# Attention 0: the input normalised by ScalarE at the head of its step, the key parts written to DRAM one step later

## The reference, cut to what matters

```python
def _layernorm(x, axis=-1, eps=1e-05):
    m = jnp.mean(x, axis=axis, keepdims=True)
    v = jnp.var(x, axis=axis, keepdims=True)
    return (x - m) / jnp.sqrt(v + eps)
...
    q = (x @ Wq).reshape(B, N, NUM_HEADS, HEAD_DIM).transpose(0, 2, 1, 3)
    k = (context @ Wk).reshape(B, M, NUM_HEADS, HEAD_DIM).transpose(0, 2, 1, 3)
    v = (context @ Wv).reshape(B, M, NUM_HEADS, HEAD_DIM).transpose(0, 2, 1, 3)
    attn = jax.nn.softmax(jnp.einsum('bhnd,bhmd->bhnm', q, k) * scale, axis=-1)
    out = jnp.einsum('bhnm,bhmd->bhnd', attn, v)
    return out @ Wo + bo
...
x = x + _L0_xattn_ref(_layernorm(x, axis=-1), ctx_1024, ...)
```

## Time and profile before

| | us |
|---|---|
| median of three runs | 829.3 (825.61 to 832.38) |
| profiled execution, its own time | 826.71 |
| span in it, first to last instruction | 824.3 |
| PE busy | 543.9 (66%) |
| DVE busy | 524.3 (64%) |
| ACT busy | 414.7 (50%) |
| POOL busy | 297.6 (36%) |

### The profile page before, as it was taken

The page is one execution under the profiler, slowest core; times in us unless marked ns, Lnnn a source line. Parts: engine busy times, 40 slices in busy tenths (PEclk is TensorE's granted clock), DMA queues, the critical chain, the costliest instruction groups (busy, mean ns, idle before and its releaser), DMA issues.

```text
span 824.3 us, 19004 instructions
## 1 busy us (share of the span) xinstructions
PE 543.9 (66%) x5619; PEld 357.2 (43%) x5619; DVE 524.3 (64%) x1608; ACT 414.7 (50%) x1037; POOL 297.6 (36%) x559
## 2 busy tenths in 40 slices
PE   5788889847888678887322432799996138793352
PEld 4576667634544454554101211455564026561131
DVE  2767676645777557776788885466775853326673
ACT  2666667733222236665435764565563014445674
POOL 2444444424555423342024326344430023323510
PEclk9999999978999759999555555599999557876555
DMA  8832333310000033432000001233330015550001
GB/s 228 212 69 62 67 64 64 69 31 0 1 0 0 18 79 91 113 96 59 10 1 0 0 0 40 53 88 89 91 91 17 0 39 142 133 137 2 0 0 52
DMA packets 102629, 47.51 MB, mean 58 GB/s; under 512 B 82160, under 2 KB 92080, under 8 KB 102448
## 3 DMA queue, kind: packets, MB, share of 16 engines
q1 hardware_dynamic: 102576, 46.87, 22.6%
HBM read 26.92 MB, written 19.92 MB: 57 GB/s over the span
## 4 chain that ended last, share of the span: by engine, by line
issue 29%; PE 20%; DVE 17%; POOL 12%; ACT 5%; DVEq 5%; DMA 5%; POOLq 3%; SPq 2%; ACTq 0%
PE bank L510 3%; DMA scratch_q<-q_parts 3%; PE bank L444 3%; POOL small L1362 2%; PE bank L459 2%; PE bank L551 2%; DMA stacks<-scratch_q 2%; POOL tmp_a L1250 2%; DVE xn L1604 2%; POOL stats L1222 2%; PE bank L476 1%; DVE small L1445 1%; DVE mx L1628 1%; PE bank L590 1%; POOL tmp_b L1250 1%
## 5 line engine op out<-in xcount | busy, mean ns | idle before, releaser
L1628 DVE TENSOR_REDUCE mx<-bank 128x4 f32<-128x512 f32 x160 | 103.8, 683 | 22.0 <-PE bank L459 20.3
L909 ACT ACTIVATE probs<-bank 128x512 f32<-128x512 f32 x160 | 90.9, 595 | 48.3 <-PE bank L480 46.2
L1283 POOL CAST q_parts<-resid 128x128 bf16<-128x128 f32 x48 | 14.2, 296 | 94.8 <-DVE resid L1643 94.8
L1643 DVE SCALAR_TENSOR_TENSOR resid<-bank,w_bias_cols,q_parts 128x128 f32<-128x128 f32 x48 | 16.8, 350 | 49.2 <-ACT q_parts L959 49.2
L510 PE MATMUL bank<-probs,v_slot 128*9 128x128 f32 x1024 | 45.9, 299 | 3.0 <-ACT probs L909 0.8
L1222 POOL TENSOR_TENSOR stats<-stats,half_neg 128x1 f32<-128x1 f32 x48 | 26.2, 546 | 57.3 <-DVE stats L1599 57.1
L1109 ACT ACTIVATE att_t<-bank 128x512 f32<-128x512 f32 x16 | 9.6, 597 | 63.8 <-PE bank L780 63.8
L476 PE MATMUL bank<-stacks 48*128 48x128 bf16 x512 | 39.6, 228 | 1.9 <-DVE shift_t L1664 1.1
L480 PE MATMUL bank<-shift_t,pick_bf 64*128 64x128 bf16 x512 | 39.4, 227 | 0.3 <-issue 0.3
L546 PE MATMUL bank<-w_ident,xn 128*128 128x128 f32 x64 | 21.4, 334 | 27.0 <-DVE xn L1604 15.8
L982 ACT ACTIVATE att<-bank 128x512 f32<-128x512 f32 (+1 forms) x48 | 25.1, 522 | 23.3 <-PE bank L510 21.5
(11 more groups left out here) (298 smaller groups left out, 1756.6 us busy)
## 6 DMA issues: line engine op xcount, KB each, us to landing
stacks<-scratch_k SPq DMA_DIRECT2D x64, 96.0 KB, 2.2
stacks<-scratch_q SPq DMA_DIRECT2D x64, 96.0 KB, 2.2
scratch_k<-k_parts SPq DMA_DIRECT2D x48, 96.0 KB, 1.9
scratch_q<-q_parts SPq DMA_DIRECT2D x48, 96.0 KB, 1.9
scratch_k<-k_parts SPq DMA_DIRECT2D x48, 64.0 KB, 1.7
scratch_q<-q_parts SPq DMA_DIRECT2D x48, 64.0 KB, 1.7
stacks<-scratch_k SPq DMA_DIRECT2D x16, 192.0 KB, 2.6
stacks<-scratch_q SPq DMA_DIRECT2D x16, 192.0 KB, 2.5
```

Source lines behind the costliest of these rows:

```text
L909: activation(probs[:, slot, :], bank[2 + u % 2][:, :], ACT.Tanh if layer == 3 else ACT.Exp, scale=float(d) ** -0.5).then_inc(sm["p"], 1)
L1628: reduce(mx[:, sM, at * UNIT:(at + 1) * UNIT], bank[u % 2][:, :].rearrange("p (h k) -> p h k", h=UNIT), AX.X, ALU.max).then_inc(sm["mx"], 1)
```

## The change

Four edits, all in attention 0:

- SP: in step t the nine writes are those of sequence t-2 instead of t-1, behind a wait for `kk_parts` of t-1 instead of t; one more emptying step is run.
- DVE: `xn_ready` is gone from the step.
- ACT: `normalized_input` is issued first in the step, ahead of `key_copied`.
- POOL: `deviation` computes for attention 0 what it does for 1 and 2 (negated mean, power, drain, product) instead of the power alone. DVE's `ln_stats` gets the wait that keeps a slot of `stats` until ACT has read it.

```diff
--- before.py
+++ after.py
@@ -325,17 +325,18 @@
                 if on(k, 0) and k >= SLOTS:
                     wait(sp, L0x["v_ps"], t - SLOTS + 1)
                     context(t, k)
-                if on(k, 1):
-                    s = (k - 1) % SLOTS
-                    wait(sp, L0x["kk_parts"], t)
+
+                if on(k, 2):
+                    s = (k - 2) % SLOTS
+                    wait(sp, L0x["kk_parts"], t - 1)
                     for l in range(3):
                         row = 0
                         for part, n in TERMS:
-                            sp.dma_start(scratch_k[l, t - 1, row:row + n].rearrange("j r k -> r j k"),
+                            sp.dma_start(scratch_k[l, t - 2, row:row + n].rearrange("j r k -> r j k"),
                                          k_parts[:, s, l, 0:n, :]).then_inc(k_saved[s], 16)
                             row += n
 
-            pipeline(sp, contexts, 1)
+            pipeline(sp, contexts, 2)
@@ -984,6 +985,7 @@
                     if layer == 0:
+                        normalized_input()
                         key_copied()
@@ -1227,7 +1229,7 @@
                     def deviation(t, k):
-                        if layer in (0, 3):
+                        if layer == 3:
                             rstd(2 * layer, t, k)
                             return
@@ -1590,7 +1592,7 @@
-                if half in (2, 4):
+                if half in (0, 2, 4):
                     wait(dve, ln["xn"], half // 2 * B + t - 3)
@@ -1705,7 +1707,6 @@
                         maximum(0)
-                        xn_ready()
                         maximum(1)
```

## The result

| | before | after |
|---|---|---|
| median of 13 runs each, us | 831.61 (825.61 to 838.76) | 835.79 (833.73 to 838.04) |
| ratio, 95% interval | | 1.0055 (1.0036 to 1.0073) |
| span of the profiled execution, us | 824.3 | 834.2 |

The kernel became slower, by 0.55%; the medians lie 4.2 us apart. That is inside the stated range. The loss is clear of the interval's scatter but small, and it is less than half of the 10.1 us that were worked out. The two profiled executions differ by 9.9 us of span, more than twice as much as the medians.

The account below looks back on a forecast made before the run. In attention 0 PE was nearest to full but waited for contexts; after the change ACT's head would wait for POOL. Steady steps +6.4 and first steps +3.7 gave +10.1 us, forecast 838 between two bases, range 827 to 843.

Parts of the forecast that it names:

- What bounds the stage: Attention 0: PE nearest to full, busy 18.3 of 21 us, waiting 10.4 us in nine steps for the late context.
- the SP edit: SP's writes in attention 0: context issued earlier, PE's wait vanishes; alone worth 0 to 9.7 us, moved writes cost nothing.
- the chain to ACT's head: Attention 0: ACT's head waits through DVE and POOL for its own line 1017; line 970 at +4.13, steady loss 6.4 us.
- The first piece of a step: Attention 0, ACT's line 1017 to line 977: 4.53 us in every step, where it was 3.95 on the mean.
- the old mean step: Attention 0 before the change: eleven steps in 108.27 us, mean 9.84, set against a forecast step of 10.42.
- the last two: Pieces of a step, line 977 to 945 and 945 to the next 1017: together 5.89 us, holding in every step.
- the first steps: Steps 0 to 4 of attention 0: delays summing to +3.7 us, bounds 0 and 4.5.
- what follows: Everything after attention 0: starts after it and moves as a whole.
- Faster: Rival, attention 0: ACT never held at its head, every step 8.96 us; gain 9.7 us, 817 or 820; chance 0.10.
- No change: Rival: first steps' 3.7 us hidden behind loads, or new path nearer its low bound; 827 to 836 us; chance 0.25.
- the forecast's +6.4 to +13: Main case: steady loss in attention 0 plus first-step delays, worked out at +10.1 us; chance 0.58.
- Slower still: Rival, POOL in attention 0: later products slip too, 0.57 us paid twice per step, 6.3 more, 844 us; chance 0.07.

Follow-up runs that it names:

- earlier statistics: Changed kernel with DVE's next-sequence statistics moved just behind the shifts and POOL's deviation ahead of its products, except every fourth sequence: 821.39 us, ratio 0.9881.
- with the earlier statistics added: Kernel before with the SP edit plus DVE's statistics and POOL's deviation moved earlier, DVE still normalising: 819.5 us, ratio 0.9852.

## Why the prediction was right in sign and too large

**What bounds the stage, the SP edit, the chain to ACT's head: right.** The first piece of a step was forecast at 4.53 and is 4.53; the step at 10.42 and is 10.39; ACT's idle time at its head at 2.7 and is 2.73. The SP edit alone is worth 818.5 against 829.59, 11.1 us, where the gap of the profiled execution gave 9.7 as an upper bound; the base was short, as below. The loss is the wait on `ln_rstd`. Taking its cause away (earlier statistics) makes the kernel 8.2 us faster than the one before on the same chip (821.39 against 829.59), moving it back in ACT's queue 2.9 (826.73 against 829.59), where the changed kernel is 4.2 slower: 12.4 and 7.0 us of its time come back.

**The rule on engine load.** The Trainium skill, Perfetto Trace Analysis, Optimizing Scalar/DVE Operations, says that moving work off DVE may make sense if DVE is saturated. The prediction read from it that here the move buys nothing, and the traces agree: DVE is busy 7.6 us less (524.3 to 516.7 on the page of the profile), and with the wait taken away the steps last 9.00 us with the move and 8.95 without it. That by engine load alone it would cost nothing either is the prediction's reading, not the page's words, and it misses the 12.4 us that the order of the queues took (the gain of the earlier statistics).

**The term that was mis-sized: the old mean step.** The prediction set 10.42 against 9.84, which is the mean of one execution, and that was a short one. Against 10.19, the mean in both later profiles, the steady steps lose (10.39 - 10.19) x 11 = 2.2 us, not 6.4; against the mean of all three profiles 3.4. The prediction's sentence that only the first piece of a step varies, with the last two at 5.89, holds for that one execution: in the five steps behind which the clock fell, the last two take 6.55 to 7.50 us. The changed kernel's step doesn't vary, since nothing in its loop waits for a DMA; the old one's did. The spread of the three runs then at hand, 825.6 to 832.4, beside a step that varied from 8.96 to 10.90 in one trace, could have said so: the prediction noted the 2.6 us to the median and split the difference, but left the step at 9.84.

**The sum by all five profiles.** On the mean of three profiles of before and two of after the steady steps cost +3.4 us, the first steps +3.2, and what follows -1.9: +4.7 us of span, beside the 4.2 us between the medians. The prediction had what follows move as a whole; it varies by 6.3 us from profile to profile, more than the change itself, so this last term may be chance.

**Luck in the time.** That 838 lies only 2.2 us above the measured 835.79 is luck. The change was 5.9 us smaller than worked out, but the base of about 828 was 3.7 below the 831.61 that thirteen runs gave, and the two errors offset each other.

**The first steps: near on the mean, but not in step 4.** Forecast +3.7 by line 1017 of step 4 (50.05 in the earlier trace rows). The first profile of after has it at 55.49, +5.4, the second at 53.41, which is +1.5 and +1.7 against the second and third profile of before; the means differ by 3.2. Steps 1, 2 and 3 came as forecast: +0.87, +0.45 and +1.25 in the second profile of after, against 0.87, 0.45 and 1.05. Where the clock fell in step 1, in the first profile, that step added 2.2 (last section). Step 4 was forecast at +0.84. It took 14.17 and 14.13 us in the changed kernel, with the clock at 0.50 for part of it, and in the kernel before 12.99 where the clock held, but 14.49 and 14.42 where it fell: like against like there is no loss.

**The rivals.** *Faster* didn't come, since line 971 starts at +4.13 and not before 2.66; the SP edit alone shows its mechanism at work, with steps of 8.99 and a time of 818.5, where this rival had 817 to 820. *No change* is the case in whose +0 to +6.4 us the measured 4.2 lies, and not the forecast's +6.4 to +13. Its mechanism is borne out only in part: the steady loss was smaller since the old steps were longer, not since the new path was shorter, and of the first steps' loss mainly that of step 4 was hidden. *Slower still* needed POOL's products to come late; they start at +1.97 as before, after 3.39 us in which POOL idled.

**A version that beats both.** The SP edit alone, 818.5 us, is 1.4% faster than the kernel before; the other three edits give that gain and more back.

## What to carry to other kernels

An engine's idle time at the head of its step is no free room: ask what the moved instruction waits for, on which engine that is made, and what stands ahead of it in that engine's queue. If the chain goes back to the same engine's tail, the idle time becomes a loop, and everything queued behind the moved instruction is on it. And before a steady step is taken from one profile, look whether a step of it depends on a DMA: such a step varies from execution to execution, and the mean of one may not be the mean.

## What was not expected of the hardware

The granted clock of PE fell to 0.50, the 1.2 GHz level, after idle stretches inside attention 0, in some executions and not in others. In the changed kernel, around the stop for the weights in step 4 (windows):

```profile
44.00:46.00 2.00, 0.66 (x6) 0.43 (x6) 1.81 (x7) 0.00 (x0) 1.04 (x1) 0.90 0.01 3
46.00:48.00 2.00, 2.00 (x17) 1.78 (x18) 1.19 (x6) 0.00 (x0) 0.56 (x2) 0.50 0.00 0
48.00:50.00 2.00, 2.00 (x15) 2.00 (x16) 1.30 (x3) 0.90 (x2) 1.36 (x4) 0.75 0.05 12
```

PE was busy for 0.66 of the 2 us in which the fall began. In step 1 of the same execution line 638 took 1.65 us and line 659 behind it 1.80, at a mean clock of 0.57 between 18 and 22 us, behind a wait of 1.11 us for the input (timeline of PE):

```profile
18.23 0.46 PE L547 MATMUL bank<-w_ident,xn 128*128 128x128 f32 x1 [1.11 <-ACT xn L971]
18.71 1.65 PE L638 MATMUL bank<-w_proj,ctx_slot 128*128 128x384 f32 x2
20.15 1.80 PE L659 MATMUL bank<-xn_t,w_wq 128*128 128x128 f32 x8
```

In its second profile the same lines, behind a wait of the same 1.11 us, ran at 1.00 (timeline of PE):

```profile
17.98 0.91 PE L638 MATMUL bank<-w_proj,ctx_slot 128*128 128x384 f32 x2
18.73 1.05 PE L659 MATMUL bank<-xn_t,w_wq 128*128 128x128 f32 x8
```

With the SP edit alone step 4 came 15.43 us after step 3, at a clock of 0.50 between 42 and 46 us; with the earlier statistics added, at 1.00 throughout, 12.58. The kernel before shows it too. In its second profile a short step of 8.95 us left SP behind with its nine writes, the next context was issued at 84.73, and PE idled for it and went on at the lower level (windows):

```profile
84.00:86.00 2.00, 0.45 (x9) 0.26 (x6) 1.85 (x8) 0.04 (x1) 1.39 (x2) 1.00 0.29 64
86.00:88.00 2.00, 1.21 (x6) 1.21 (x7) 1.48 (x4) 0.00 (x0) 1.86 (x4) 0.72 0.07 19
88.00:90.00 2.00, 2.00 (x11) 2.00 (x11) 0.00 (x0) 0.89 (x2) 0.09 (x1) 0.50 0.40 82
```

The timeline of the same place:

```profile
84.73 0.37 SPq L312 DMA_DIRECT2D ctx_slot<-in_ctxT  x1
...
86.79 2.03 PE L630 MATMUL bank<-ctx_slot,w_wk 128*128 128x128 f32 x8 [2.34 <-DMA ctx_slot<-in_ctxT]
```

The keys took 2.03 us instead of the 1.15 of the earlier trace rows, and that step lasted 12.76. Beside the short step of 8.95 that is 3.81 more, of which 2.34 are the wait itself. A late context thus costs its wait and, where the clock fell behind it, 1.1 to 2.5 us more in the five steps of this kind; that may be why taking the wait away was worth more than the 9.7 us that the first profile showed. The length of the wait alone doesn't tell the two apart. Behind the first of these waits, in the first profile, the clock held; behind the second, in the second profile, it fell (timeline):

```profile
122.94 1.15 PE L630 MATMUL bank<-ctx_slot,w_wk 128*128 128x128 f32 x8 [2.02 <-DMA ctx_slot<-in_ctxT]
127.35 1.66 PE L630 MATMUL bank<-ctx_slot,w_wk 128*128 128x128 f32 x8 [1.88 <-DMA ctx_slot<-in_ctxT]
```

Why the clock fell in some executions and held in others after stops of much the same length stays open; no run here took it apart.
